# A mixed eight-layer transformer on one core: filled waits on TensorE, a reordered feed-forward pipeline, and an earlier block table

## What is computed

```python
x = x + layernorm(sublayer(layernorm(x)))
```

```python
hid = gelu(h @ W1[e] + b1[e])                 # 256 x 256
r = hid @ W2[e] + b2[e]                       # 256 x 128
out = h + 0.3 * (r @ Wo + bo)
```

## Time and profile before

| | us |
|---|---|
| median of 3 runs | 1131.25 |
| lowest, highest | 1130.49, 1139.63 |
| the profiled execution | 1135.26 |
| its span, first to last instruction | 1133.4 |
| experts 0, to its last early block (180.8 to 250) | 69.2 |
| feed-forward 1 (542.8 to 587.5) | 44.7 |
| feed-forward 2 (876.3 to 922.3) | 46.0 |
| stage 3 before its slots (922.3 to 1016) | 93.7 |

### The profile page before, as it was taken

The page is one execution under the profiler, slowest core; times in us unless marked ns, Lnnn a source line. Parts: engine busy times, 40 slices in busy tenths (PEclk is TensorE's granted clock), DMA queues, the critical chain, the costliest instruction groups (busy, mean ns, idle before and its releaser), DMA issues. The chain is left out here.

```text
span 1133.4 us, 23807 instructions
## 1 busy us (share of the span) xinstructions
PE 930.7 (82%) x7973; PEld 726.8 (64%) x7988; DVE 725.7 (64%) x2000; ACT 572.4 (51%) x1192; POOL 464.1 (41%) x528
## 2 busy tenths in 40 slices
PE   6899895699993789889779999999997767539990
PEld 5566664689983655655667666767666655428990
DVE  4678645676665866774557667666644668856664
ACT  2667662346652576765354555454442445325662
POOL 2366663563444212221361333343343442575442
PEclk9899996799996998999799999999999977658995
DMA  9211110121212112111400011111021620012214
GB/s 294 69 53 52 52 54 1 41 72 47 58 29 75 39 59 59 59 58 42 138 27 1 2 40 40 40 39 32 10 57 21 239 85 1 21 54 66 60 46 111
DMA packets 80767, 66.42 MB, mean 59 GB/s; under 512 B 6706, under 2 KB 73457, under 8 KB 80267
## 3 DMA queue, kind: packets, MB, share of 16 engines
q1 hardware_dynamic: 76139, 56.45, 17.5%
q0 software_dynamic: 4512, 8.47, 2.2%
HBM read 38.76 MB, written 26.58 MB: 58 GB/s over the span
## 5 line engine op out<-in xcount | busy, mean ns | idle before, releaser
L454 DVE TENSOR_REDUCE a_rowmax<-a_banks 128x4 f32<-128x1024 f32 (+1 forms) x112 | 136.7, 1222 | 58.9 <-PE a_banks L721 27.3
L2378 POOL TENSOR_TENSOR a_both<-a_probs 128x512 f32<-128x512 f32 x64 | 86.3, 1348 | 159.8 <-ACT a_probs L2603 159.8
L576 ACT ACTIVATE a_probs<-a_banks 128x1024 f32<-128x1024 f32 x112 | 115.0, 1026 | 58.2 <-PE a_banks L707 47.2
L1243 POOL DMA_INDIRECT acc<-m_result,m_yb x77 | 75.5, 980 | 96.4 <-DVE m_result L1560 52.6
L2603 ACT ACTIVATE a_probs<-a_banks 128x1024 f32<-128x1024 f32 x64 | 65.6, 1025 | 88.5 <-PE a_banks L2662 88.5
L2509 DVE TENSOR_REDUCE a_rowmax<-a_banks 128x4 f32<-128x1024 f32 x64 | 78.0, 1220 | 15.0 <-PE a_banks L2639 14.9
L1236 POOL DMA_INDIRECT rows<-m_yrow,m_idx x64 | 64.7, 1010 | 45.6 <-issue 21.1
L1673 ACT ACTIVATE m_gate<-m_banks 128x352 f32<-128x352 f32 (+1 forms) x93 | 42.9, 461 | 72.7 <-PE m_banks L1862 72.7
L2676 PE MATMUL a_banks<-a_probs,a_V 128*64 128x256 f32 x512 | 69.4, 392 | 0.6 <-ACT a_craw L2592 0.6
L1888 PE MATMUL m_banks<-e_down,m_hT_hi 128*128 (+2 forms) x231 | 65.3, 351 | 0.6 <-DVE m_hT_lo L1543 0.6
L749 PE MATMUL a_banks<-a_probs,a_V 128*32 128x256 f32 x720 | 59.2, 401 | 6.9 <-ACT a_raw L564 6.4
(11 more groups left out here) (382 smaller groups left out, 2746.0 us busy)
## 6 DMA issues: line engine op xcount, KB each, us to landing
rows<-fill SPq DMA_DIRECT2D x16, 520.0 KB, 4.3
a_factor<-recip_rows SPq DMA_DIRECT2D x28, 256.0 KB, 4.6
rows<-fill SPq DMA_DIRECT2D x15, 455.0 KB, 4.0
m_yb<-rows SPq DMA_DIRECT2D x77, 65.0 KB, 1.8
f_expert<-in_experts SPq DMA_DIRECT2D x16, 257.5 KB, 3.0
m_parts<-acc SPq DMA_DIRECT2D x16, 256.0 KB, 5.0
e_gu_lo<-in_gu SPq DMA_DIRECT2D x1, 2736.0 KB
e_last_row<-in_last_rows SPq DMA_DIRECT2D x1, 2736.0 KB
```

The lines of the kernel that those rows point to most:

```text
L454: nc.vector.reduce_max(o, src, AX).then_inc(rowmax_ready, 1)
L576: nc.scalar.activation(probs[h][:, k, :, :], ps[:, 4:6, :], ACT.Exp, scale=SCALE).then_inc(exp_done, 1)
L1243: nc.gpsimd.indirect_dma_start(acc.rearrange("k n d -> (k n) d"), bass.IndirectOffsetOnAxis(yb[b % YB][:, P:P + 1].bitcast(U32), 0), resul ...
L2378: nc.gpsimd.tensor_tensor(both[u % 4][:, :, :], p[:, :, 0, :], p[:, :, 1, :], ALU.add).then_inc(both_ready, 1)
```

## The change

Three edits, none of which alters the result.

1. In both experts stages TensorE gets identity matmuls, `keep_busy(n, bank)`, ahead of waits. In layer 0: 4 in `ranks(0)` and 7, 8 and 10 in the norm events of runs 1, 2 and 3. In layer 3, run 3 only: 6 in `channel_scores`, 18 in `channel_values`, 28 in the norm event, 16 in `ranks`, and 4 ahead of the first slot. The waits that guard the PSUM bank are moved ahead of them.
2. The feed-forward stage is reordered. The input moments are taken for two sequences at a time and all eight sequences are normed before the output sums begin; eight buffers y and yT replace three and two; the bias is added in place (yb is gone). TensorE turns sequences 0 to 3 in the prologue and s + 5 in step s, and issues first(s + 1) ahead of second(s). The final normalization moves from ScalarE (one activation with a shift that VectorE prepared) to VectorE (`tensor_scalar`), and the shift is gone.
3. In stage 3 the late table stands after two slots (-2, -1).

```diff
@@ mixed_events
-    return events + [("slot", s) for s in slots[:4]] + [("map", 0)] + [("slot", s) for s in slots[4:]]
+    return events + [("slot", s) for s in slots[:2]] + [("map", 0)] + [("slot", s) for s in slots[2:]]
@@ experts, tensor
+            def keep_busy(n, b):
+                for _ in range(n):
+                    mm(ps[:, b, 0:P], g.ident[:, :], g.ident[:, :], start=True, stop=True)
             def channel_scores(r):
+                if r == RUNS - 1:
+                    keep_busy(6, 0)
                 pe.wait_ge(c_qk_ready, r + 1)
             def channel_values(r):
+                if r == RUNS - 1:
+                    keep_busy(18, 0)
                 pe.wait_ge(c_zn_ready, r + 1)
             def ranks(r):
-                pe.wait_ge(one_hot_ready, r + 1)
+                if by_distance and r == RUNS - 1:
+                    keep_busy(16, 0)
                 if by_distance and r + 2 < RUNS:
                     pe.wait_ge(c_top_ready, r + 3)
                 if not by_distance and r + 1 < RUNS:
                     pe.wait_ge(yT_ready, r + 2)
+                    pe.wait_ge(logits_read, r + 1)
+                    if r == 0:
+                        keep_busy(4, 7)
+                pe.wait_ge(one_hot_ready, r + 1)
                 if kind == "norm":
-                    pe.wait_ge(y_ready, r + 1)
                     if r >= 1:
                         pe.wait_ge(yT_ready, r)
                     if not by_distance:
                         if r >= 1:
                             pe.wait_ge(logits_read, r)
+                            keep_busy((7, 8, 10)[r - 1], 7)
+                    elif r == RUNS - 1:
+                        keep_busy(28, 7)
+                    pe.wait_ge(y_ready, r + 1)
                     if r == -2 and by_distance:
+                        keep_busy(4, 0)
                         pe.wait_ge(spot_ready, RUNS)
@@ selected_ffn, gpsimd
-            in_power(0)
-            in_power(1)
+            in_power(0)                       # now two sequences each
             ...
-            in_power(2)
+            in_power(1)
             pool.wait_ge(bo_ready, 1)
             with_bias(0)
             with_bias(1)
-            for s in range(SEQS + 4):
+            in_power(2)
+            with_bias(2)
+            in_power(3)
+            for s in range(SEQS + 3):
                 if s + 3 in ahead:
-                    in_power(s + 3)
-                if s + 2 in ahead:
-                    with_bias(s + 2)
+                    with_bias(s + 3)
...
-                if s - 3 in ahead:
-                    i = s - 3
+                if s - 2 in ahead:
+                    i = s - 2
                     pool.wait_ge(t_ready, i + 1)
@@ selected_ffn, vector
-            for s in range(SEQS + 3):
-                if s + 2 in ahead:
-                    normed(s + 2)
-                if s + 3 in ahead:
-                    in_moments(s + 3)
+            normed(2)
+            normed(3)
+            for k in (2, 3):
+                in_moments(k)
+                normed(2 * k)
+                normed(2 * k + 1)
+            for s in range(1, SEQS + 2):
...
-                    nc.vector.scalar_tensor_tensor(shift[:, i, :], mv["out"][:, i, :, 0], -1.0, rstd["out"][:, i, :],
-                                                   ALU.mult, ALU.mult).then_inc(shift_ready, 1)
+                    if i >= 2:
+                        dve.wait_ge(x_done, i - 1)
+                    for j in range(T):
+                        last = nc.vector.tensor_scalar(t[i % 2][:, j, :], f[i % 3][:, j, :], mv["out"][:, i, j, 0:1],
+                                                       rstd["out"][:, i, j:j + 1], ALU.subtract, ALU.mult)
+                    last.then_inc(t_ready, 1)
@@ selected_ffn, scalar
+            for i in range(1, 4):
+                to_sbuf(i)
+            hidden(0)
+            to_sbuf(4)
+            for s in range(SEQS):
                 if s + 1 in ahead:
-                    to_sbuf(s + 1)
+                    hidden(s + 1)
+                if s + 5 in ahead:
+                    to_sbuf(s + 5)
+                act.wait_ge(r_ps, s + 1)      # then the bias activation, as before
@@ selected_ffn, tensor
-            busy(12)
+            turned(1)
+            busy(5)
+            turned(2)
+            turned(3)
+            busy(5)
+            first(0)
+            turned(4)
             for s in range(SEQS + 1):
+                if s + 1 in ahead:
+                    first(s + 1)
+                if s - 1 in ahead:
+                    output(s - 1)
+                if s + 5 in ahead:
+                    turned(s + 5)
                 if s in ahead:
+                    second(s)
             busy(26)
```

More of the change, by code:

```diff
@@ L2000, in selected_ffn @@
         last_var, last_rstd = st.sb("last_var", [SEQS, 1]), st.sb("last_rstd", [SEQS, 1])
-        y = [st.sb(f"y{k}", [P, T, P]) for k in range(3)]
-        yb = [st.sb(f"yb{k}", [P, T, P]) for k in range(2)]
-        yT = [st.sb(f"yT{k}", [P, SEQ]) for k in range(2)]
+        y = [st.sb(f"y{k}", [P, T, P]) for k in range(SEQS)]
+        yT = [st.sb(f"yT{k}", [P, SEQ]) for k in range(SEQS)]
         hT = [st.sb(f"hT{k}", [P, 2, SEQ]) for k in range(2)]
@@ L2084, in _, with moments @@
             nc.vector.tensor_scalar(bo[:, :], at["bo"], 0.3, None, ALU.mult).then_inc(bo_ready, 1)
-            def moments(k, i, src, done):
-                for j in range(T):
-                    last = nc.vector.bn_stats(stats[k][:, i, j, :], src(j))
+            def moments(k, of, src, done):
+                for i in of:
+                    for j in range(T):
+                        last = nc.vector.bn_stats(stats[k][:, i, j, :], src(i, j))
                 steps.after(last)
@@ L2162, in to_sbuf, with hidden @@
                 act.wait_ge(yT_ps, i + 1)
+                nc.scalar.activation(yT[i][:, :], ps[:, i % 2, 0:SEQ], ACT.Copy).then_inc(yT_ready, 1)
+            def hidden(i):
+                act.wait_ge(expert_loaded[i], 16)
+                act.wait_ge(h_ps, i + 1)
                 if i >= 2:
-                    act.wait_ge(h_ps, i - 1)
-                nc.scalar.activation(yT[i % 2][:, :], ps[:, i % 2, 0:SEQ], ACT.Copy).then_inc(yT_ready, 1)
+                    act.wait_ge(r_ps, i - 1)
+                for c in range(2):
+                    last = nc.scalar.activation(hT[i % 2][:, c, :], ps[:, 2 + i % 2, c * SEQ:(c + 1) * SEQ], ACT.Gelu,
+                                                bias=ex[i]["b1"][:, c:c + 1])
+                last.then_inc(h_ready, 1)
             act.wait_ge(y_lastT_ps, 1)
@@ new lines, in _, with first, output @@
+            turned(1)
[3 more added lines that the diff above has]
+            busy(5)
+            def first(i):
+                pe.wait_ge(expert_loaded[i], 16)
+                pe.wait_ge(yT_ready, i + 1)
+                for c in range(2):
+                    last = mm(ps[:, 2 + i % 2, c * SEQ:(c + 1) * SEQ], ex[i]["w1"][:, c * P:(c + 1) * P], yT[i][:, :],
+                              start=True, stop=True)
+                last.then_inc(h_ps, 1)
+            def output(i):
+                pe.wait_ge(r_ready, i + 1)
+                if i >= 2:
+                    pe.wait_ge(f_ready, i - 1)
+                for j in range(T):
+                    last = mm(ps[:, 6 + i % 2, j * P:(j + 1) * P], rT[i % 2][:, j * P:(j + 1) * P], at["wo"], start=True,
+                              stop=True)
+                last.then_inc(out_ps, 1)
@@ new lines, in second @@
+            def second(i):
+                pe.wait_ge(h_ready, i + 1)
+                for c in range(2):
+                    last = mm(ps[:, 4 + i % 2, 0:SEQ], ex[i]["w2"][:, c * P:(c + 1) * P], hT[i % 2][:, c, :], start=c == 0,
+                              stop=c == 1)
+                last.then_inc(r_ps, 1)
+            first(0)
+            turned(4)
+            for s in range(SEQS + 1):
+                if s + 1 in ahead:
[4 more added lines that the diff above has]
+                    turned(s + 5)
+                if s in ahead:
+                    second(s)
```

105 lines of the change are left out of this document (26 added, 79 removed).

## The result

| | before | changed |
|---|---|---|
| median, us (8 runs each) | 1134.28 | 1122.03 |
| lowest, highest | 1130.49, 1141.25 | 1118.83, 1126.58 |
| the profiled execution | 1135.26 | 1120.89 |
| its span | 1133.4 | 1119.2 |

The ratio of the changed kernel to the one before is 0.9877, with a 95% interval from 0.9848 to 0.9907: 14.0 us of 1134.28 (10.5 to 17.2). The two medians are 12.3 apart, the two profiled spans 14.2. The forecast was 16 and 1115; it started from 1131.25, the median of the first 3 runs, and with 8 runs the kernel before stands at 1134.28. So of the 6.8 us between 1115.25 (1131.25 - 16) and 1122.03, 3.0 are the starting point and 3.7 the gain. 1122.03 lies on the upper edge of the stated range of 1108 to 1122, 0.03 beyond it, and outside the 1110.5 to 1119.5 of case A.

What follows compares the result with a forecast made beforehand. Bounds: a TensorE-ScalarE loop in feed-forward, VectorE, ScalarE and GpSimd chains in the experts stages, TensorE in stage 3's slots. Feed-forward 8.6, table 4.4, fillers 2 and 1.5 sum to 16.5, held to 16: 1131.25 to 1115, range 1108 to 1122.

Steps and rivals of the forecast that it cites:

- case A: Whole kernel: every part acts about as counted, 1110.5 to 1119.5 us, likeliest 1115; chance 0.62.
- feed-forward 1: First feed-forward stage: the reorder ends it 4.6 us earlier.
- feed-forward 2: Second feed-forward: same steps plus identity matmuls at 5.97 rather than 7.19, 5.8 us, of which 5.5 taken.
- late weights and clock taken off: Stage 3's first use waits for weights, 0.5 us; waiting for turned(4) may cost both feed-forwards the clock, 1.0 in all.
- late table: Stage 3: 1.90 us wait and 3.2 of half clock saved, less 0.7 delay: 4.4 us net.
- fillers, experts 0: Experts 0: about half the possible half-clock savings, less overshoot, gains 2 us; bounds -2.7 and 5.
- fillers, stage 3: Stage 3: fillers fit their waits and work behind may get full clock, 1.5 us; bounds -2 and 4.
- the wait for norm(4): Feed-forward start: turned(4) queues ahead of first(1) and needs norm(4), ready about 555.4; the start costs 1.2 us.
- The pitch: Feed-forward loop: TensorE alone sets the pace, 0.97 second, 0.87 first and 0.50 output, 2.34 us a sequence.
- Rival B: Feed-forward: VectorE and GpSimd become the bound, 2.77 us a sequence, each stage gains some 2.5 less: 1120; chance 0.15.
- C: Experts stages: TensorE's clock falls to half between filler and next work; fillers 0, table 2.5: 1120 us; chance 0.10.
- Rival E: Feed-forward: TensorE's queue stands at turned(4) and turned(6) for VectorE; slower, 1134 us; chance 0.04.

Runs made afterwards that it cites:

- p_fill3: The kernel before with only the identity matmuls of the last stage (72 calls over five places of the last run); ratio to the kernel before 1.0022.
- a_table0: The full change with the late table of experts 0 one place sooner, directly behind the last send; ratio to the kernel before 0.9947.
- a_second: The full change with TensorE's second(s) ahead of the turn, now of sequence s + 4, and ScalarE's copies to match; ratio to the kernel before 0.9896.
- a_actnorm: The full change with the feed-forward's final normalization back on ScalarE, three steps behind, and VectorE's shift with it; ratio to the kernel before 0.9889.
- p_table: The kernel before with only the late table of the last stage two places sooner; ratio to the kernel before 0.9977.
- a_again: The full change measured again on another chip, nothing else altered; ratio to the kernel before 0.9932.
- b_fill: The full change with second(s) ahead of the turn and 21 instead of 26 identity matmuls ending each feed-forward; median 1119.23, ratio to the kernel before 0.9840.
- b_table0: The kernel b_fill with the late table of experts 0 one place sooner, directly behind the last send; ratio to the kernel before 0.9891.
- p_fill0: The kernel before with only the identity matmuls of layer 0's experts stage; ratio to the kernel before 1.0029.
- p_ffn: The kernel before with the feed-forward reorder alone; ratio to the kernel before 0.9911.

## Why the prediction was right, and where it was off

**Sizes of the terms**, in us, from the profile; the first six lines are the sum of the prediction:

| term | forecast | measured |
|---|---|---|
| feed-forward 1 | 4.6 | 5.1 |
| feed-forward 2 | 5.5 | 6.0 |
| late weights and clock taken off | -1.5 | 0 |
| late table | 4.4 | 4.6 |
| fillers, experts 0 | 2.0 | 3.4 |
| fillers, stage 3 | 1.5 | 0.3 |
| stages without a change | 0 | -4.6 |
| rest: 0.3 gained up to the first matmul, 0.3 lost in attention 2, 0.6 behind the slots' first blocks | 0 | -0.6 |

The first six lines make 16.5 and 19.4, the whole 14.2 (with rounding). The parts gained more than forecast; the 16 was missed by a term that wasn't in the sum. That the median fell at the edge of the range is in part luck: 2.9 more from the parts, 5.2 less from stages outside the sum, and a starting point 3.0 higher, which nothing in the runs ties together. Each size in the table is the difference of one pair of executions.

**Feed-forward: right, with each step near.** Less the 0.95 us by which the trace is shifted, the wait for norm(4) ended at 555.35 (forecast 555.4), second(0) started at 556.71 (556.9), the wait for norm(6) ended at 559.93 (560.2), second(2) started at 562.60 (563.0). The pitch was 2.17 to 2.18 instead of 2.34: the `second` costs 0.87, not 0.97, because it no longer begins after a wait, and an `output` 0.44, not 0.50. The earlier trace rows doesn't show the 0.50; in the kernel before, too, the next instruction stood 0.44 behind the output of 560.49. That is the mis-sized term: the duration of an instruction that follows a wait, used for a pipeline without waits, and a 0.50 that no row gives. The group of 26 began at 32.75 us into the stage (forecast 33.3) and was the stage's end, as said. In feed-forward 2 it took 5.97 instead of 7.19, as forecast. Over all profiles this group of 26 took 7.2 to 7.6 us in four of the eight feed-forwards in the old order, 5.97 in the other four, and 5.97 in every one in the new order. So the 1.2 belongs to most executions and not to all: p_fill3's second feed-forward, in the old order, took 45.00 us and not 46.70. What was taken off for the clock and for the weights was not needed in this profile: stage 3's first turn came 5.15 us after its first matmul, as before, and the clock in feed-forward 1 stayed at 1.00 behind 552.5. The weights are close, though: in a_table0, whose feed-forwards are those of the full change, VectorE waited 2.12 us for them and that turn came at 6.37. In a_second, 1.75 and 1.35 us of the start's loss came back, so pricing TensorE's queue at turned(4) and turned(6) was right, and it was the part's main cost.

**Rival B, the shared port: there, and small.** Norms 2 and 3, and again 6 and 7, took 1.94 us for four instructions that take 1.2 alone, each time beside two of GpSimd's biases (1.4); norms 4 and 5 took 1.51 beside one. The prediction allowed 0.7 for such a pair; it was 0.74, 0.31 and 0.74. Taken singly, an instruction that met a bias took 0.75 to 0.76 us and ended within 0.1 us of it, the others 0.33 to 0.34. At the start this mattered: 0.74 in norms 2 and 3 and 0.4 in the first instruction of norm(4) lie ahead of TensorE's wait of 0.88 for norm(4), so without them that wait would have been gone (an estimate from these rows). In the pipeline it never set the pace (a_actnorm: 2.17 to 2.18 us a sequence either way): there the final normalization lies beside the power and kept its 0.60. The last one, beside a residual of 0.72, took 1.00:

```profile
579.55 1.00 DVE L2173 TENSOR_SCALAR f_t<-f_f,f_out_mv,f_out_rstd 128x128 f32<-128x128 f32 x2 [0.34 <-POOL f_out_rstd L2090]
...
579.50 0.72 POOL L2095 TENSOR_TENSOR x<-x,f_t 128x256 f32<-128x256 f32 x1
```

The Trainium skill's rule that was weighed ("SBUF — State Buffer", "SBUF: two separate sides") agrees with the norms beside a bias or a residual, 1.94 beside 1.41 and 1.00 beside 0.72. As the prediction put it, for any instruction of the two engines, it doesn't hold: beside the power of 0.73 the normalization took what it takes alone.

**Late table: right in place and side effects, and in size for this pair.** 4.6 instead of 4.4, a wait of 0.77 at the turn of block 3 (about 1 was said), half clock until 1009.9 and then 1.00, no wait for block 9. The three later profiles on a chip without standing point to 3.1 to 3.5. On chips on which ScalarE stands the same move gains what p_table shows, 2.7 us with an interval from a gain of 6.7 to a loss of 1.4.

**Fillers: the weakest term, as said, and wrong in its split.** Experts 0 gained 3.4, inside the bounds of -2.7 and 5. Of it, 0.8 was there by the turn of run 3 (36.67 us into the stage instead of 37.50), and the rest came between it and the scores of run 3, in slots that ran at 1.00 (0.50 in the earlier trace rows). The later profiles bear out the second part, at 1.3 to 2.5, and not the 0.8. The overshoot was 0.2 us for the groups of 7 and 8 and none for the 10, against 0.4, 0.8 and 1.5: the group of 10 ran at full clock, 2.47 us. In stage 3 the wrong step is "They begin slow and end fast, so they fit", and that the work behind them "may be granted 1.00". 28 calls took 6.50 us, the wait behind them was still 5.91, and the turn of run 3 took 1.12, which is half clock: C, at this place and in this execution. In eight profiles with fillers in stage 3 that turn took 1.11 to 1.12 in five and 0.66 in three (a_again, b_fill, b_table0), so the same code does both. But it hardly matters: the turn of block 0 came at 90.34 us into the stage in a_again, with the 0.66, at 90.70 in the full change, with the 1.12, and at 90.41 in p_table, without any filler. The gain was 0.3 because GpSimd and the rows set the chain, as the prediction warned.

**What was missing: the clock of stages that don't change.** The prediction carried the difference of one profiled execution over to the median. Attention 1 alone moves by 10 us between executions, more than any term of the sum, and attention 0 by 7. A sum of stage gains is right for the stages and not for one pair of executions; the range should have carried some 4 us for it.

**Rival E** (TensorE's queue at the turns, slower) was priced with the right place: the waits were 0.88 and 0.89 us, far from the 4.6 us from which it decides.

## What to carry to other kernels

Compare stage by stage, from each stage's first matmul, before explaining a total: here the changed stages gave 18.8 us, and unchanged ones took back 4.6 by their clock, in a way that the next execution does otherwise. The size of a part's gain scatters too; one pair of profiles gives it to 1 or 2 us at best. In a hand-written queue put the instruction whose input is ready ahead of the one that will wait (`second` ahead of the turn gave 1.4 to 1.8 us a stage for moving two lines), and take the durations for a pipeline without waits from rows that don't follow a wait. When a stage gets shorter, look at the loads of the next one: 0.9 to 1.5 us of the fastest kernels' gain went into waiting for them. A filler is worth its place only if the engines behind it take up what the faster clock gives; measure that per stage, and on more than one chip.

## What the runs showed of the hardware that wasn't expected

- The granted clock differs over the same instructions with the same waits: 1.00 and 0.58 over 20.5 us of attention 1. Attention 1 took 178.75 to 188.88 us in 14 profiles, attention 0 172.46 to 179.69; attention 2 took 288.7 to 289.2 in all of them.
- A VectorE normalization of 128x128 took 0.75 us beside a GpSimd add of 128x256 and 0.33 beside a GpSimd power of 128x2 (0.73 us) or alone.
- The chips differ in the experts stages. In nine of the profiles experts 0 took 193.7 to 198.1 us and stage 3 213.7 to 219.6; in the five others 176.4 to 181.4 and 206.0 to 210.4. Attention 2 is the same on all. In each of the nine, ScalarE has 4 to 8 gaps of 2 to 10 us in these two stages for which the profile gives no plausible releaser; each overlaps indirect transfers that GpSimd issues. In the five others there is no such gap. In the two that were followed through, its input had been ready for 4.1 us (222.07 of p_fill0) and through all of 4.7 (1037.72 of p_ffn). Its cause stays open; no run here changes ScalarE's code or the sends.
